# Expert routing moved batch by batch into the attention of layer 2

## What is computed

```
x = x + tanh(g_xattn[2]) * attention(layernorm(x), ctx, ctx)     # 32 query heads of 16, 8 key heads
x = x + tanh(g_ffn[2])   * moe(layernorm(x))                     # 8 experts, 2 for each token

logits = xf @ router_w.T                      # 2048 x 8
topk_vals, topk_idx = top_k(logits, 2);  topk_w = softmax(topk_vals)
y1 = x_sorted @ w1[expert];  y_act = silu(gate) * up;  y2 = y_act @ w2[expert]     # hidden 352
y = sum over a token's two experts of y2 * topk_w
```

## Time and profile before

| | us |
|---|---|
| median of three runs | 4111.81 |
| profiled execution, own time | 4112.18 |
| its span, first to last instruction | 4110.3 |
| PE busy | 3674.0 (89%) |
| DVE busy | 1980.3 (48%) |
| ACT busy | 1371.9 (33%) |
| POOL busy | 368.4 (9%) |
| mean granted clock of TensorE | 0.951 |

### The profile page before, as it was taken

One profiled execution on the slowest core, in us unless ns is written; L12 is line 12 of the kernel. 1 busy time (PEld: TensorE's weight loads), 2 busy tenths in 40 slices (PEclk: granted clock), 3 DMA queues, 4 the chain that ended last, 5 costly groups with the idle time before them and its releaser, 6 DMA issues.

```text
span 4110.3 us, 35816 instructions
## 1 busy us (share of the span) xinstructions
PE 3674.0 (89%) x11778; PEld 1702.4 (41%) x11779; DVE 1980.3 (48%) x3525; ACT 1371.9 (33%) x2823; POOL 368.4 (9%) x387
## 2 busy tenths in 40 slices
PE   1999999965679998379978999999999998999999
PEld 0444444422344444146633444444444443444443
DVE  8656565143777765211126766656666562111111
ACT  5524342010246666022223434434434341001000
POOL 7000000000222220221110000000000000000000
PEclk6999999988889999689989999999999999999999
DMA  2322212200302321345561111000000002222221
GB/s 115 123 83 83 97 67 72 102 25 9 72 29 56 74 55 20 155 128 164 162 213 55 44 45 35 24 35 24 35 35 23 35 12 72 72 88 86 77 86 52
DMA packets 77384, 291.57 MB, mean 71 GB/s; under 512 B 10424, under 2 KB 11320, under 8 KB 66236
## 3 DMA queue, kind: packets, MB, share of 16 engines
q1 hardware_dynamic: 68928, 264.12, 19.6%
q0 software_dynamic: 8320, 25.71, 2.0%
HBM read 255.68 MB, written 33.59 MB: 70 GB/s over the span
## 4 chain that ended last, share of the span: by engine, by line
PE 78%; DVE 10%; issue 6%; ACT 3%; DMA 1%; POOL 1%; SPq 0%; DVEq 0%; ACTq 0%; POOLq 0%
PE BM L2009 6%; PE BM L2064 5%; PE BM L529 5%; PE BR L529 5%; PE BR L2073 4%; PE BM L364 4%; PE BR L364 4%; PE BS L2047 3%; PE BT L1349 3%; PE BS L545 3%; PE BT L545 3%; PE BT L2056 3%; PE BR L1694 3%; PE BM L2022 3%; PE BM L1683 2%
## 5 line engine op out<-in xcount | busy, mean ns | idle before, releaser
L2138 ACT ACTIVATE AR<-BS,AR 128x512 f32<-128x512 f32 x256 | 174.4, 685 | 411.8 <-DVE AR L2233 411.8
L2132 ACT COPY AR<-BM 128x512 f32<-128x512 f32 x340 | 198.8, 585 | 305.9 <-PE BM L2064 99.9
L2246 DVE SCALAR_TENSOR_TENSOR X<-BR,AR,X 128x512 f32<-128x512 f32 x256 | 191.9, 750 | 205.4 <-PE BR L2073 196.1
L2233 DVE TENSOR_REDUCE AR<-BS 128x2 f32<-128x1024 f32 x128 | 157.0, 1226 | 252.8 <-PE BS L2047 252.8
L2073 PE MATMUL BR<-AR 128*128 128x512 f32 x512 | 255.6, 623 | 4.2 <-DVE X L2246 0.6
L2064 PE MATMUL BM<-AR 128*128 128x512 f32 x512 | 246.1, 593 | 0.0
L364 PE MATMUL BM<-XT,AR 128*128 (+1 forms) x512 | 233.1, 598 | 4.8 <-DMA AR<-l_w_dram 4.8
L2009 PE MATMUL BM<-XT,AR 128*128 128x512 f32 x512 | 236.6, 605 | 0.7 <-ACT XT L239 0.7
L529 PE MATMUL BM<-XT,AR 128*128 128x512 f32 x512 | 230.6, 593 | 0.9 <-ACT AR L632 0.9
L364 PE MATMUL BR<-XT,AR 128*128 (+1 forms) x512 | 230.2, 592 | 0.0
L529 PE MATMUL BR<-XT,AR 128*128 128x512 f32 x512 | 230.2, 592 | 0.0
(11 more groups left out here) (335 smaller groups left out, 5982.3 us busy)
## 6 DMA issues: line engine op xcount, KB each, us to landing
AR<-l_w_dram SPq DMA_DIRECT2D x128, 512.0 KB, 3.5
AR<-l_wq_dram SPq DMA_DIRECT2D x32, 1152.0 KB, 5.2
AR<-l_w_dram SPq DMA_DIRECT2D x42, 768.0 KB, 4.8
AR<-w2h SPq DMA_DIRECT2D x16, 1024.0 KB, 4.8
QS<-qx SPq DMA_DIRECT2D x32, 512.0 KB, 9.7
AR<-l_w_dram SPq DMA_DIRECT2D x16, 1024.0 KB, 4.8
AR<-l_w_dram SPq DMA_DIRECT2D x8, 1408.0 KB
made<-AR SPq DMA_DIRECT2D x40, 256.0 KB, 4.8
```

What stands on the lines that cost most here:

```text
L2132: nc.scalar.copy(to, BM[:, L3[job] % 2, :]).then_inc(m_free, 1)
L2246: nc.vector.scalar_tensor_tensor(out=xb, in0=BR[:, L3[job] % 2, :], scalar=RS3[:, p % 2, h, st:st + 1], in1=xb, op0=ALU.mult, op1=ALU.add) ...
```

## The change

A batch's expert choice moves into the attention of the batch after it; only batch 3 stays behind the attention.

- **Constants** (router, triangle, token numbers, a row of priorities and bases) are loaded at the attention's start, into the last 848 words of the work area. The maxima's staging tile MTS is halved: its two buffers lie on different partitions, and the logits on a third place.
- **Norms.** The next batch's norm (jobs "n") is spread: statistics one tile at a time in group 0, rows in group 1, turned tiles one per key tile in groups 1 and 2. From batch 1 on a second norm is made, of the batch that has just been finished (jobs "q"): statistics in group 2, rows in group 3, turned tiles in groups 3 and 4; SP stores its rows in group 5, ahead of the next keys and queries.
- **Routing**, from batch 1 on, for the batch before: router matmuls at the end of group 4 ("lg"), turn back in group 5 ("lt"), DVE's choice in two pieces in group 5, ranks at the start of group 6 ("rk"), running counts and places in two pieces in group 6, POOL's scatters in groups 6 and 7.
- **The table** has one stretch of 2048 places for each expert, so a place can be given before later batches are counted. At the end POOL gathers from it the 128-number rows that belong to the tiles, PE turns them and DVE copies them: that is the list of slots. What depends on all counts (tile starts, places of results, pair weights) stays behind the attention.
- **Weights.** Experts 0, 1 and 7 are loaded in the last three groups of the attention, where their memory is free; experts 2 to 6 and the second weights behind it. The second weights of the first tile's expert are loaded when the first gather has landed.

```diff
@@ tables and small pieces, ahead of the attention
+        def route_best(v, mx, of, oh):
+            tt = nc.vector.tensor_tensor
+            link(v, nc.vector.tensor_reduce(mx, of, op=ALU.max, axis=AX.X))
+            link(v, tt(EQ, of, one(mx, E), ALU.is_ge))
+            link(v, tt(EQ, EQ, per_e(PRIO, ST), ALU.mult))
+            link(v, nc.vector.tensor_reduce(MS, EQ, op=ALU.max, axis=AX.X))
+            link(v, tt(oh, EQ, one(MS, E), ALU.is_equal))
+        def route_first(v, lg):
+            route_best(v, MX0, lg, OH0)
+            link(v, nc.vector.scalar_tensor_tensor(out=LG2, in0=OH0, scalar=-1.0e30, in1=lg, op0=ALU.mult, op1=ALU.add))
+        def route_second(v, b):
+            route_best(v, MX1, LG2, OH1)
+            nc.vector.tensor_tensor(OHS, OH0, OH1, ALU.add).then_inc(ohs_ready, 1)
+            link(v, nc.vector.tensor_tensor(EX[:, b * ST:(b + 1) * ST], MX1, MX0, ALU.subtract))
+        def route_carry(v, b, ranks):
+            link(v, nc.vector.tensor_copy(PREF[:, 0, :], PREF[:, ST, :] if b else BASE))
+            for t in range(ST):
+                link(v, tt(PREF[:, t + 1, :], PREF[:, t, :], ranks[:, ST + t, :], ALU.add))
+            link(v, tt(RT[:, 0:ST, :], ranks[:, 0:ST, :], PREF[:, 0:ST, :], ALU.add))
+        def route_place(v, b, oh, idx):
+            link(v, nc.vector.tensor_tensor(EQ, oh, RT[:, 0:ST, :], ALU.mult))
+            link(v, nc.vector.tensor_reduce(POS, EQ, op=ALU.add, axis=AX.X))
+            nc.vector.tensor_copy(idx[:, b * ST:(b + 1) * ST], POS).then_inc(idx_ready, 1)
+            v.wait_ge(idx_ready, 2 * b + (1 if idx is IDX0 else 2))
+        def scatter_tokens(pool, b, j):
+            pool.wait_ge(idx_ready, 2 * b + j + 1)
+            for tile in range(b * ST, (b + 1) * ST):
...
+        EARLY, ON_TIME = (0, 1, E - 1), tuple(range(2, E - 1))
+        N_SLOTS = ((1, 2), (1, 3), (2, 0), (2, 1))
+        Q_SLOTS = ((3, 3), (4, 0), (4, 1), (4, 2))
+        R_SLOTS = ((4, 3), (5, 0), (6, 0))
@@ l2_sync
+                for dst, src in ((RW, l2_router), (EC, moe_row...), (TRI, moe_tri), (TOK, moe_token)):
+                    sp.dma_start(dst, src).then_inc(router_in, 16)
...
+                if g == 5 and b:
+                    store_rows(sp, b - 1)
+                if n >= NG - 3:
+                    if n == NG - 3:
+                        sp.wait_ge(e_full, L2["e", NG - 5, 3, 3] + 1)
+                    up_weights(sp, EARLY[n - NG + 3])
                 if g == 4 and b < B - 1:
                     store(b + 1)
@@ l2_tensor (l2_scalar has a copy for each job in the same places)
-                    if n % KVH == 1 and tt == 3:
-                        turn_norm(n // KVH)
+                    for job in l2_extra(n, tt):
+                        if job[0] in "nq":
+                            turn_norm(*job)
+                        if job[0] == "lg":
+                            logits(job[1])
+                        if job[0] == "lt":
+                            back(job[1])
+                        if job[0] == "rk":
+                            ranks(job[1])
@@ l2_vector, called behind each maximum, slot = 2 * tt + half
-                    if n % KVH == 0 and tt == 3:
-                        norm_begin((n // KVH + 1) % B)
-                    if n % KVH == 1 and tt == 1:
-                        norm_end((n // KVH + 1) % B, n // KVH)
+            def beside(n, slot):
+                b, g = divmod(n, KVH)
+                st, late = divmod(slot, 2)
+                if g == 0 and b < B - 1 and late:
+                    norm_stats_of(b + 1, st)
+                if g == 1 and b < B - 1 and slot < ST:
+                    norm_rows(b + 1, slot, ...)
+                if b and g == 2 and late:
...
+                    norm_stats_of(b - 1, st)
+                if b and g == 3 and 1 <= slot <= ST:
+                    norm_rows(b - 1, slot - 1, ...)
+                if b and g == 5 and slot == 2:
+                    v.wait_ge(lg_ready, b)
+                    route_first(v, LG)
+                if b and g == 5 and slot == 4:
+                    route_second(v, b - 1)
+                if b and g == 6 and slot == 3:
+                    v.wait_ge(rt_ready, b)
+                    route_carry(v, b - 1, RT)
+                if b and g == 6 and slot == 5:
+                    route_place(v, b - 1, OH0, IDX0)
+                    route_place(v, b - 1, OH1, IDX1)
@@ l2_pool
+            pool.wait_ge(router_in, 64)
...
+                if routed_batch(n, 2) is not None:
+                    norm_pool(pool)
+                if routed_batch(n, 6) is not None:
+                    scatter_tokens(pool, routed_batch(n, 6), 0)
+                if routed_batch(n, 7) is not None:
+                    scatter_tokens(pool, routed_batch(n, 7), 1)
@@ moe_sync
+            for e in ON_TIME[:2]:
+                up_weights(sp, e)
+            sp.dma_start(EW2[1], l2_w2[0]).then_inc(ew2_in[1], 16)
+            store_rows(sp, B - 1)
+            for e in ON_TIME[2:]:
+                up_weights(sp, e)
             sp.wait_ge(routed, 1)
...
-            down(1, 0)
+            sp.wait_ge(xg_in[0], 16)
             down(0, 0)
@@ moe_pool
+            norm_pool(pool)
             nc.gpsimd.memset(EHT, 0.0).then_inc(e_zero, 1)
...
+            for j in range(2):
+                scatter_tokens(pool, B - 1, j)
+            pool.wait_ge(row_ready, 1)
+            pool.wait_ge(table_in, 2 * B * ST * 16)
+            nc.gpsimd.indirect_dma_start(out=SLT, out_offset=None, in_=table.rearrange("(r n) o -> r (n o)", n=P),
+                                         in_offset=bass.IndirectOffsetOnAxis(ap=ROW, axis=0)).then_inc(slt_in, 16)
+            pool.wait_ge(slots_ready, 1)
             pool.wait_ge(xnd_in, B * 16)
```

More of the change, by code:

```diff
@@ new lines, in route_logit, with turn_logits, route_ranks @@
+        def route_logit(bank, half, kt):
+            return nc.tensor.matmul(bank[0:E, :], RW[:, kt, :], XT[:, half, kt, :], start=kt == 0, stop=kt == KT - 1)
+        def turn_logits(bank):
+            for st in range(ST):
+                last = nc.tensor.transpose(bank[:, st * E:(st + 1) * E], LT[:, st * P:(st + 1) * P], ID[64:64 + E, 64:64 + E])
+            return last
+        def route_ranks(bank):
+            n = ST * E
+            ohs = OHS.rearrange("p t e -> p (t e)")
+            nc.tensor.matmul(bank[:, 0:n], TRI, ohs, start=True, stop=True)
+            return nc.tensor.matmul(bank[:, n:2 * n], ONE, ohs, start=True, stop=True)
@@ L1475, in norm_begin, with norm_rows @@
                 nc.vector.tensor_scalar(VAR[:, :], MV[:, :, 1], EPS_BLOCK, None, ALU.add).then_inc(norm_var, 1)
[L1477 to L1487, removed]
+            def norm_rows(b, st, used, stored=0):
+                if st == 0:
+                    if used is None:
+                        v.wait_ge(turn.free, T_V.now() + 2)
+                    else:
+                        v.wait_ge(e_full, L2[used] + 1)
+                    if stored:
+                        v.wait_ge(xnd_in, 16 * stored)
+                    v.wait_ge(norm_rstd, N_V.now() + 1)
+                last = nc.vector.tensor_scalar(XN[:, st, :], X[:, 4 * b + st, :], MV[:, st, 0:1], RSTD[:, st:st + 1], ALU.subtract, ALU.mult)
+                if st == ST - 1:
+                    last.then_inc(xn_ready, 1)
+                    N_V.step()
@@ L1710, in moe_scalar @@
                 act.sem_inc(q.free, 2)
-            for b in range(B):
-                nc.scalar.copy(LT[0:E, :], full(act, em, m)[0:E, :]).then_inc(em.free, 1)
-                if b < B - 1:
-                    norm_scalar(act, (b + 1) & 1)
+            norm_scalar(act, 0)
+            nc.scalar.copy(LT, full(act, em, m)[0:E, :]).then_inc(lt_ready, 1)
+            act.wait_ge(lt_ready, B)
+            act.sem_inc(em.free, 1)
             act.wait_ge(pair_exp_in, 1)
@@ L1827, in moe_vector @@
+            nc.vector.tensor_copy(SLOTS, full(v, er, r)[:, 0:TW]).then_inc(slots_ready, 1)
+            v.wait_ge(slots_ready, 1)
+            v.sem_inc(er.free, 1)
+            m.step()
             with loop(v, NT // 2, (m, 2), (r, 4)) as i:
```

350 lines of the change are left out of this document (203 added, 147 removed).

## The result

The changed kernel takes **4055.99 us**, the median of four runs (4051.71 to 4059.43), against 4112.15 in the same session (four runs): a ratio of **0.9864, 95% interval 0.9849 to 0.9879**. It is faster by 56 us where 79 were forecast. The profiled execution took 4057.63 us (span 4055.8), 54.5 less than that of before.

The account below looks back on a forecast made before the run. Prediction: latency bounds the stretch from attention to first expert matmul, TensorE the attention. Gain 86.5 behind the attention less 7.8 lost inside it is 78.7; 4112.2 - 78.7 = 4033 us, range 4016 to 4064.

Parts of the forecast that it names:

- sign: Whole kernel: faster; chance 0.95 of faster by more than 8 us, 0.01 within that, 0.04 slower.
- the likeliest case: Whole kernel: the forecast itself, net gain 78.7 us, giving 4033 us; chance 0.80.
- The way: Last attention add to first expert matmul: 130.2 us falls to 43.7, a gain of 86.5.
- a small loss in the attention: Inside the attention: 40.6 us of work added, 32.8 removed, a loss of 7.8; bounds -9 and +46.
- the forecast's upper bound of the gain: Behind the attention: router matmuls at full clock (3.60 instead of 5.37), shorter ranks and a 1.72 landing give 90 us.
- the forecast's own 2.1: Attention, DVE's routing steps: 2.1 us of the 5.3 per batch passes on to the pace, 6.4 for three batches.
- the 0.4: Attention: share of DVE's 25 routing steps per batch (5.3 us) taken to pass on to the pace.
- the first rival: Attention: every DVE routing and norm step stops PE and passes on in full, 18.5 us more, 4052; chance 0.12.
- DVE's pieces in full: Attention: every DVE routing and norm step stops PE, which waits for score banks, 18.5 us more, 4052; chance 0.12.
- POOL late: Attention: adds and maxima queue behind POOL's scatters, PE waits 5.0 at six places, 30 us more, 4063; chance 0.04.
- The clock: Attention: small waits hold the granted clock at its lower level, up to +216 us, 4250; chance 0.04.
- The early loads: Three expert weight loads issued in the attention's last groups: costed at nothing, covered by the scatter; without it worth 10 us.

Follow-up runs that it names:

- the spaced kernels: The changed kernel with each place of its table given 16 or 64 bytes instead of 4: 4036.81 and 4036.77 us; variants add further edits.

## Why the prediction was right or wrong

**Right: sign, range and the likeliest case.** The way was to be bought by a small loss in the attention, and so it was. 4055.99 lies within 4016 to 4064, but in the part that belonged to the rivals, by a cause that was none of them: that the range held is luck.

**The step that failed** is "Eight scatters where 32 stood: 7 x 1.26 + 0.3 + 2.13 to land = 11.3". The issue is right: eight, 1.26 apart. The landing was taken from a row whose writes went to other addresses, as if it were a property of the scatter; the change moves those too, by its new table, and the forecast put that at nothing without a reason. With the loads out of the way the landing stayed (15.51), with other addresses it went back to 2.2. From the last place to the landing it took 24.2 us (1681.61 to 1705.83), 12.9 more. The forecast named a landing over 7 as what would prove it wrong, and it was 14.88.

**The same cause in the attention.** "POOL: four scatters (5.0) go between one group's maxima and the next group's add; ... so nothing" asked only how long POOL is busy. POOL was indeed early enough; what came late were the rows of maxima on SP's queue. With the landing restored the attention gives 9.2 us back. The trace fits the Trainium skill here (DMA: Bandwidth & Descriptors, Queues, rings and completion order): a DMA engine's increment of a semaphore lands only after all earlier writes of that engine, from whichever of its queues. By that rule a 16 KB transfer on SP's queue is told late behind POOL's scatters although its data are there. The transfer's packets had ended at 1403.40, its last event came at 1412.6, and the scatters' events came all that while. Which DMA engine each of these events belongs to is not shown.

**The rest, by its own steps**, in the changed kernel's chain: norm 7.0 where 6.3 was taken (the clearing beside the rows is part of it); transposes and router matmuls 7.3 instead of 9.2, since the router matmuls ran at 3.54 and not near 5.37, as the forecast's upper bound of the gain had it (4.72 with places of 16 bytes, so this varies with the granted clock); copy and turn 1.1, choice 2.7 for 2.6, ranks 1.1 for 1.0, carry and place 1.96 for 1.95; the gather of the table 3.9 with its start, for 3.5; its transpose and copy 0.9; the token gather 3.5 for 3.6; to the first matmul 2.4 for 2.3. With places of 16 bytes the whole way is 44.7 for the forecast 43.7.

The attention with places of 16 bytes loses 8.9 us from the first group's copy to the last, for 7.8. In it groups 5 and 6 stand 2.9 above two plain ones, of which 0.8 was for turn and ranks: if these cost that, 2.1 is left for DVE's steps, the forecast's own 2.1. So the 0.4 fits for 25 steps, but not as a share: the run with 20 more passed on 16.4 us for 11.5 of DVE's work. There the first rival, and the rule of the Trainium skill behind it (VectorE: DVE Perf Modes, Rules for kernel authors), hold.

**Rivals.** DVE's pieces in full: in groups 4 to 6 PE waits for DVE 0.6 us at a time at most. POOL late: no wait for it in any group. The clock: 0.99 over the 28 groups, as before; it fell only behind the wait for the maxima. The early loads are worth nothing that the median shows, as forecast. But the forecast took it that loads which fit into the way cost nothing there; they fit, and cost the scatter beside them 2.9.

**Balance** of the profiled executions, against -78.7: way -74.1 for -86.5; attention +18.1 for +7.8; what lies before, between and behind these two +1.5 together, for 0. Sum -54.5. The part behind the first expert matmul also differs by 3 us among the spaced kernels, so this last term is open.

## What to carry to other kernels

The landing of the scatters of 4-byte numbers here went by the addresses, not by the instruction: when a change lays out the target anew, the old row is no price for it. Give each number 16 bytes: that cost nothing here. Keeping parallel lists off equal offsets took most of the landing away too, and one more DVE step for each list of results' places. Ask of every late completion who else is told late with it: the slow scatters cost 11.4 us on their own queue and 9.2 on another. And look at packets and semaphore events apart: a transfer whose packets are late stands behind others, one whose packets have long ended waits for its completion.

## What the runs showed of the hardware that was not expected

- Scatters of 128 numbers of 4 bytes, written side by side into eight lists 8192 bytes apart, land 14.88 us after the last issue; 16 bytes apart 2.21; side by side at 8704 bytes 5.94. The packets end within 1.8 us in all three; what differs is how long behind them the completion is told: 13.1, 0.4 and 4.1 us.
- While such scatters are open, small transfers on another queue are told up to 11 us after issue (2.5 beside scatters of spaced numbers), though their packets have ended, and weight loads that start then move 45 GB/s over their first 4 us at a DMA share of 0.94, 166 without.
- The Trainium skill (DMA: Bandwidth & Descriptors, Latency and other measured facts) tells of copies that lose speed when their rows in memory lie large powers of two apart, 512 KB and more, and regain it with 4 KB of padding. No run here shows such copies. Single numbers are slow here at 8192 bytes, and 512 bytes of padding take most of it away; whether the cause is the same was not tried.
- Weight loads at full rate beside a scatter of spaced numbers raise its landing from 2.21 to 5.06, and there it is the packets that are late (4.5 us after the issue instead of 1.8).
